# A fixed low-pass gate and four implicit convolution layers: 3x3 convolutions on sixteen 32x32 tiles in place of four 128x32 tiles

## The reference

```
Kj = K[j] - mean of each 3x3 kernel;  Lj likewise
z = conv3x3(x, Kj);  z = relu(batchnorm(z))       # "conv1"
x = x + 0.1 * conv3x3T(z, Kj)                     # "conv2"
x = batchnorm(x)
x = ifft2(fft2(x) / (0.1 * |fft2(Lj)|^2 + 1))     # "Fourier"
```

## Time and profile before

| what | us |
|---|---|
| median of 3 runs (lowest, highest) | 797.01 (794.98, 799.77) |
| the profiled execution, its own time | 796.84 |
| its span, first to last instruction | 795.0 |
| PE busy | 748.3, 94% of the span |
| DVE, ACT, POOL busy | 497.3, 449.3, 95.5 |
| share of the chain that ended last, on PE | 84% |
| of it line 873, the convolutions | 40% |

### The profile page before, as it was taken

The page is one execution under the profiler, slowest core; times in us unless marked ns, Lnnn a source line. Parts: engine busy times, 40 slices in busy tenths (PEclk is TensorE's granted clock), DMA queues, the critical chain, the costliest instruction groups (busy, mean ns, idle before and its releaser), DMA issues.

```text
span 795.0 us, 14900 instructions
## 1 busy us (share of the span) xinstructions
PE 748.3 (94%) x6016; PEld 375.6 (47%) x6016; DVE 497.3 (63%) x911; ACT 449.3 (57%) x703; POOL 95.5 (12%) x92
## 2 busy tenths in 40 slices
PE   4788999999999999999999999999999999999993
PEld 1222333222455875324558752345587632455782
DVE  2568787765957853449578534496686333966761
ACT  0456666636745765267357652683576625826773
POOL 0357766830000000000000000000000000000000
PEclk9789999999999999989999999899999998999997
DMA  9991111248000132830000328400004273000045
GB/s 184 189 153 28 28 29 28 55 91 187 2 1 1 33 77 68 193 98 2 1 1 18 93 57 191 112 1 1 2 7 103 55 183 88 1 1 2 1 100 113
DMA packets 60133, 51.16 MB, mean 64 GB/s; under 512 B 53153, under 2 KB 53282, under 8 KB 58018
## 3 DMA queue, kind: packets, MB, share of 16 engines
q1 hardware_dynamic: 54690, 48.92, 28.7%
q10 hardware_dynamic: 5376, 1.30, 1.1%
HBM read 11.92 MB, written 4.19 MB: 20 GB/s over the span
## 4 chain that ended last, share of the span: by engine, by line
PE 84%; DVE 8%; ACT 2%; issue 2%; DMA 1%; SPq 1%; POOL 0%; DVEq 0%; ACTq 0%; POOLq 0%
PE psum L873 40%; PE psum L1054 7%; PE psum L1025 7%; PE psum L947 6%; PE psum L1043 6%; PE psum L1009 5%; PE psum L896 3%; PE psum L998 3%; DVE spare L810 2%; PE psum L973 2%; PE psum L935 2%; DVE work L810 2%; PE psum L912 1%; DVE tabT L794 1%; PE psum L1018 1%
## 5 line engine op out<-in xcount | busy, mean ns | idle before, releaser
L873 PE MATMUL psum<-Z,wts 128*32 128x512 f32 x1536 | 176.7, 613 | 1.9 <-DVE Z L787 1.9
L873 PE MATMUL psum<-X,wts 128*32 128x512 f32 x1536 | 170.1, 593 | 0.2 <-DMA X<-X 0.2
L810 DVE COPY work<-psum 64x256 f32<-64x256 f32 x224 | 100.3, 448 | 22.8 <-PE psum L1009 15.9
L720 DVE BATCH_NORM_STATS2 stats<-Z 128x6 f32<-128x512 f32 x60 | 41.6, 693 | 102.2 <-ACT Z L470 101.8
L873 PEld LDWEIGHTS psum<-Z,wts 128*32 128x32 f32 x1536 | 48.9, 112 | 116.4 <-issue 107.8
L470 ACT ACTIVATE Z<-psum 128x512 f32<-128x512 f32 x64 | 38.2, 598 | 113.2 <-PE psum L873 102.1
L873 PEld LDWEIGHTS psum<-X,wts 128*32 128x32 f32 x1536 | 47.5, 109 | 105.4 <-issue 103.0
L555 ACT ACTIVATE work<-psum 64x256 f32<-64x256 f32 x160 | 83.1, 519 | 22.4 <-PE psum L1043 15.4
L530 ACT ACTIVATE Z<-Z,small 64x128 f32<-64x128 f32 (+3 forms) x92 | 84.8, 972 | 5.2 <-DVE small L778 4.7
L801 DVE SCALAR_TENSOR_TENSOR X<-psum,X 128x512 f32<-128x512 f32 x64 | 43.8, 684 | 46.6 <-PE psum L873 46.2
L542 ACT ACTIVATE work<-psum 128x512 f32<-128x512 f32 x64 | 61.1, 1108 | 8.9 <-PE psum L998 8.8
(11 more groups left out here) (104 smaller groups left out, 897.0 us busy)
## 6 DMA issues: line engine op xcount, KB each, us to landing
X<-X SPq DMA_DIRECT2D x64, 260.0 KB, 3.8
Z<-Z SPq DMA_DIRECT2D x32, 520.0 KB, 7.1
Z<-x SPq DMA_DIRECT2D x36, 128.0 KB, 4.8
out<-Z SPq DMA_DIRECT2D x60, 64.0 KB, 1.9
parS<-par SPq DMA_DIRECT2D x4, 673.0 KB, 8.2
Z<-x SPq DMA_DIRECT2D x12, 120.0 KB, 4.9
Z<-x ACTq DMA_DIRECT2D x14, 64.0 KB, 4.3
Z<-x SPq DMA_DIRECT2D x14, 64.0 KB, 4.6
```

The lines of the kernel that those rows point to most:

```text
L810: last = nc.vector.tensor_copy(dst, src)
L873: last = nc.tensor.matmul(out_b[C * r:C * r + C, :], weights[:, o:o + C], rows(src, reg, bp, g, CH, dj - 1), start=(dj == 0), stop=(dj == ...
```

## The change

**Tiles.** A convolution is done in 32x32 tiles, sixteen at a time: row quadrant q of the input times column quadrant r of the output, one tap per matmul. A block is four pieces of w groups each (w = 4, 2 or 1, so 512, 256 or 128 columns), in four banks. Its nine taps are nine passes; in each pass the four pieces (k) use different row quadrants, so that no two row tiles write the same bank and quadrant. The passes come in three phases of three column shifts. `PHASES` names for each phase and piece the copy (0 plain, 1 shifted by one row) and the row tap. Between phases PE waits for its own last matmul (the semaphore `through`), except that the one piece that stays on its tiles (`stays`) has its first pass ahead of the wait. A block is 144 matmuls, each again two pairs of instructions. Its four banks are claimed together and filled together.

**Copies and weights.** X2 and Z2 become X1 and Z1, shifted by one row: one DMA of 96 partitions and one of 32. The weights are plain taps, made by two DVE operations in place of four; the masks and windows go from the constants and from par.

**Blocks.** Conv1 of layer 0 has ten blocks: eight of w = 1 at prologue chunks 5 to 12 and two of w = 4 behind the prologue. Later conv1: w = 4, 4, 4, 2, 2. Conv2: w = 2, 2, 4, 4, 4. DVE's and ACT's work follows the pieces, so there are four copies or adds per block, of 128, 256 or 512 columns, and the last four conv1 pieces have their statistics taken from PSUM.

**Order.** The list of the layer's steps is new, and now also holds DVE's and ACT's own steps (`stats`, `relu`, `squares`, `table_sum`, `invert`, `scales`, `prepare`, `taps`). The reciprocal is cut in two of 512 columns. DVE moves eight of sixteen fwdW and eight of sixteen invH chunks (before: twelve and six). The ReLU of pair 0 is cut at group 9 instead of 4, that of the other pairs is one piece. In the last layer invH of pair 3 stands between invW of pairs 2 and 3. The prologue's own steps are as before.

```diff
--- before.py
+++ after.py
...
-BEHIND = 5
+CONV1_FIRST = [(bp, g, 1) for bp in range(2) for g in range(0, G, 4)] + [(2, 0, 4), (3, 0, 4)]
+CONV1 = [(0, 0, 4), (1, 0, 4), (2, 0, 4), (3, 0, 2), (3, 8, 2)]
+CONV2 = [(0, 0, 2), (0, 8, 2), (1, 0, 4), (2, 0, 4), (3, 0, 4)]
+AMONG = {i + 5: [i] for i in range(8)}
+LATE = [i for i in range(len(CONV1_FIRST)) if all(i not in some for some in AMONG.values())]
...
+def pieces_of(stage, j, some=None):
+    blocks = plan(stage, j) if some is None else [plan(stage, j)[i] for i in some]
+    return [(bp, g + n * k, n) for bp, g, n in blocks for k in range(4)]
...
+PHASES = (((0, 0), (0, 1), (1, 0), (1, -1)), ((0, 1), (1, -1), (0, -1), (1, 1)), ((1, -1), (1, 0), (0, 1), (0, 0)))
+def quadrants(phase, k):
+    shifted, di = PHASES[phase][k]
+    return (di - shifted) % R
+def stays(phase, k):
+    return phase > 0 and quadrants(phase, k) == quadrants(phase - 1, k)
...
+FWDW_DVE = [(bp, q) for bp in range(BP) for q in range(0, Q, 2)]
+INVH_DVE = [(bp, q) for bp in range(BP) for q in range(1, Q, 2)]
 def layer_steps(j):
-    first, second = range(0, 2), range(2, 4)
-    steps = [("table", j, 0), ("table", j, 1), ("norm", j, 1), ("table", j, 2), ("table", j, 3)]
-    after = {
-        5: fourier(j, 0, "turn"),
-        7: fourier(j, 0, "fwdW"),
-        9: fourier(j, 0, "fwdH") + fourier(j, 1, "turn"),
-        11: fourier(j, 0, "invH") + fourier(j, 1, "fwdW"),
-        13: fourier(j, 1, "fwdH") + fourier(j, 2, "turn"),
-        15: fourier(j, 1, "invH") + fourier(j, 2, "fwdW"),
-    }
-    for c in range(NCH):
-        steps += [("conv2", j, c)] + after.get(c, [])
-    steps += fourier(j, 3, "turn") + [("norm", j, 2)] + fourier(j, 2, "fwdH")
-    steps += fourier(j, 0, "invW") + fourier(j, 3, "fwdW") + fourier(j, 2, "invH") + fourier(j, 1, "invW")
-    steps += fourier(j, 3, "fwdH")
-    rest = {1: fourier(j, 3, "invH"), 3: fourier(j, 2, "invW"), 5: fourier(j, 3, "invW")}
-    for c in range(NCH):
-        if j + 1 < DEPTH:
-            steps.append(("conv1", j + 1, c))
-        steps += rest.get(c, [])
+    f = lambda what, bp: fourier(j, bp, what)
+    conv2 = lambda i: conv_steps("conv2", j, [i])
+    stats = lambda i: [("stats", j, i)]
+    conv1 = lambda i: conv_steps("conv1", j + 1, [i]) if j + 1 < DEPTH else []
+    prepare, taps = ([("prepare", j + 1)], [("taps", j + 1)]) if j + 1 < DEPTH else ([], [])
+    steps = [("table", j, 0), ("table", j, 1), ("squares", j, 0), ("norm", j, 1), ("table", j, 2), ("table", j, 3)]
+    steps += [("relu", j, 0, 0), ("squares", j, 1), ("relu", j, 0, 1), ("table_sum", j), ("relu", j, 1, 0)]
+    steps += conv2(0) + stats(0) + conv2(1) + stats(1) + [("relu", j, 2, 0), ("invert", j, 0)] + conv2(2) + stats(2)
+    steps += f("turn", 0) + [("invert", j, 1), ("relu", j, 3, 0)] + conv2(3) + f("fwdW", 0) + stats(3) + f("turn", 1)
+    steps += conv2(4) + f("fwdH", 0) + f("fwdW", 1) + stats(4) + f("turn", 2)
+    steps += f("invH", 0) + [("norm", j, 2)] + f("fwdH", 1) + [("scales", j)] + f("fwdW", 2) + prepare + f("turn", 3)
+    steps += f("invW", 0) + f("invH", 1) + f("fwdH", 2) + f("fwdW", 3) + f("invW", 1) + f("invH", 2) + f("fwdH", 3)
+    steps += conv1(0) + f("invW", 2) + f("invH", 3) + conv1(1) + taps + f("invW", 3)
+    for i in range(2, len(CONV1)):
+        steps += conv1(i)
     return steps
...
+RELU_CUTS = {0: [0, 9, G]}
+FIRST_SLOTS = (0, 1)
...
-        def shift_two(eng, dst, src, bp, done, h=None):
-            s, d, n = bp * REG, bp * REG2, G * GROUP
+        def shift_one(eng, dst, src, bp, done, h=None):
+            s, d, n = bp * REG, bp * REG1, G * GROUP
             if h is not None:
                 n //= 2
                 s, d = s + n * h, d + n * h
-            eng.dma_start(dst[0:2 * C, d + GROUP:d + GROUP + n], src[2 * C:128, s:s + n]).then_inc(done, 16)
-            eng.dma_start(dst[2 * C:128, d:d + n], src[0:2 * C, s:s + n]).then_inc(done, 16)
+            eng.dma_start(dst[0:3 * C, d + GROUP:d + GROUP + n], src[C:128, s:s + n]).then_inc(done, 16)
+            eng.dma_start(dst[3 * C:128, d:d + n], src[0:C, s:s + n]).then_inc(done, 16)
...
-                if c == NCH - 1:
-                    act.wait_ge(last_stats, j + 1)
-                nc.scalar.activation(rows(Z0, REG, c // Q, CH * (c % Q), CH), by_row(bank(n)),
+            def keep_conv1(j, bp, g, w):
+                n = NUMBER["conv1", j, bp, g, w]
+                bk.full(n)
+                if (bp, g, w) in pieces_of("conv1", j)[-4:]:
+                    act.wait_ge(last_stats, 4 * j + 1 + pieces_of("conv1", j)[-4:].index((bp, g, w)))
+                nc.scalar.activation(rows(Z0, REG, bp, g, w), by_row(bank(n)[:, 0:ROW * w]),
...
-                    for form in range(2):
-                        o = (2 * k + form) * 3 * C
-                        w = wts[:, o:o + 3 * C].rearrange("p (d o) -> p d o", o=C)
-                        m = ksum[:, C * k:C * k + C].unsqueeze(1).broadcast_to([128, 3, C])
-                        f = parS[:, P_F + o:P_F + o + 3 * C].rearrange("p (d o) -> p d o", o=C)
-                        last = nc.vector.scalar_tensor_tensor(w, in0=m, scalar=cstS[:, C_MASK + form:C_MASK + form + 1],
-                                                              in1=f, op0=ALU.mult, op1=ALU.add)
+                    o = k * TAPS * C
+                    w, f = (t[:, o:o + TAPS * C].rearrange("p (t o) -> p t o", o=C) for t in (wts, parS[:, P_K:P_GB]))
+                    m = ksum[:, C * k:C * k + C].unsqueeze(1).broadcast_to([128, TAPS, C])
+                    last = nc.vector.scalar_tensor_tensor(w, in0=m, scalar=-1.0 / TAPS, in1=f, op0=ALU.mult, op1=ALU.add)
...
+                late = i - len(pieces_of("conv1", j)) + 4
+                if late >= 0:
                     bk.full(n)
-                    nc.vector.bn_stats(stats[:, 6 * c:6 * c + 6], bank(n)).then_inc(last_stats, 1)
-                    dve.wait_ge(last_stats, j + 1)
+                    nc.vector.bn_stats(stats[:, 6 * i:6 * i + 6], bank(n)[:, 0:ROW * w]).then_inc(last_stats, 1)
+                    if late == 3:
+                        dve.wait_ge(last_stats, 4 * j + 4)
...
+                z = rows(Z1, REG1, 0, FIRST_SLOTS[1], RELU_CUTS[0][1] - FIRST_SLOTS[1])
...
+            def invert(j, i):
+                dve.wait_ge(table_summed, j + 1)
+                t = tabT[:, N * i:N * i + N]
+                nc.vector.reciprocal(t, t).then_inc(table_done, 1)
...
+            def conv2_stats(j, i):
+                for k, (bp, g, w) in enumerate(pieces_of("conv2", j, [i])):
+                    bk.result(NUMBER["conv2", j, bp, g, w])
+                    o = 6 * (4 * i + k)
+                    last = nc.vector.bn_stats(stats[:, o:o + 6], rows(X0, REG, bp, g, w))
+                if i == len(CONV2) - 1:
+                    link(last)
+                    aggregate("conv2", j)
...
-            def conv(n, c, X, X2_, weights):
-                bp, q = divmod(c, Q)
-                bk.claim(n)
-                out_b = bank(n)
-                for dj in range(3):
-                    for r in range(R):
-                        form, src, g = ((1, X2_, CH * q), (0, X, CH * q), (1, X, CH * q), (0, X2_, CH * q + 1))[r]
-                        reg = REG2 if r in (0, 3) else REG
-                        o = form * 3 * C + dj * C
-                        last = nc.tensor.matmul(out_b[C * r:C * r + C, :], weights[:, o:o + C],
-                                                rows(src, reg, bp, g, CH, dj - 1), start=(dj == 0), stop=(dj == 2),
-                                                tile_position=(0, C * r))
-                last.then_inc(filled[n % BANKS], 1)
-            def conv1(j, c):
-                if c == 0:
+            passed = []
+            def conv(step, X, XS, weights):
+                stage, j, bp, g0, w = step
+                ns = [NUMBER[stage, j, bp, g0 + w * k, w] for k in range(4)]
+                for n in ns:
+                    bk.claim(n)
+                for phase in range(3):
+                    order = sorted(range(4), key=lambda k: not stays(phase, k))
+                    for dj in range(3):
+                        for k in order:
+                            if phase and dj == 0 and k == [k for k in order if not stays(phase, k)][0]:
+                                pe.wait_ge(through, len(passed))
+                            shifted, di = PHASES[phase][k]
+                            for r in range(R):
+                                q = (r + quadrants(phase, k)) % R
+                                src, reg = (XS, REG1) if shifted else (X, REG)
+                                g = g0 + w * k + shifted + (r + di - shifted) // R
+                                tap = C * (3 * (di + 1) + dj)
+                                last = nc.tensor.matmul(bank(ns[k])[C * r:C * r + C, 0:ROW * w], weights[C * q:C * q + C, tap:tap + C],
+                                                        rows(src, reg, bp, g, w, dj - 1, C * q, C * q + C),
```

(75 more changed lines are left out.)

179 lines of the change are left out of this document (89 added, 90 removed).

## The result

The changed kernel takes 915.4 us (median of 4 runs, 909.27 to 917.19) against 796.0 us (median of 4, 792.29 to 799.77): ratio 1.149, 95% interval 1.141 to 1.156. It is slower by 119 us; the prediction was 757.0 us (729 to 787).

A forecast was written before the change was run, and what follows sets the result against it. The prediction took PE to be the bound, busy 748.3 of 795.0 us. Layers 0 to 2 (-32.7), layer 3 and the end (-10.5) and the prologue (+4.3) summed to -38.9 us from 796.84: 757 us, range 729 to 787.

The forecast's parts named there:

- rival (a): Convolution passes: a floor that width doesn't lower, from instruction starts or weight loading; +112, 869 us; chance 0.10.
- A pass of 512 columns stays 0.863 us: Convolution blocks: with sixteen tiles a pass keeps its time, so w = 4 streams for 9 x 0.863 = 7.77 us.
- the term of 8.47: Convolutions: time in us of one w = 4 block, nine passes of 0.863 plus hand-overs of 0.35.
- Blocks of w = 2 cost 4.58 us, of w = 1 2.64: Convolutions: narrow blocks stream for 3.88 and 1.94 us, plus hand-overs between phases.
- Blocks of w = 1 cost nothing: Prologue: such a block costs 2.64 us where a chunk costs 2.59; extra copies and statistics are covered.
- The shift DMAs move the same bytes and are early: Shifted copies in the layers: DMAs are early by a whole convolution; no cost counted.
- Hand-over 0.35 us: Between a block's phases: PE's wait for itself, 0.35 us each, bounds 0.10 and 0.60, 90 hand-overs.
- Norm 1 +1.45: Between conv1 and conv2, layers 1 to 3: statistics in four pieces and a longer first ReLU, +1.45 us each.
- New waits, +1.4 a layer: Layers: PE waits of 1.2, 1.0 and 0.8 us, less the present 1.6; net +1.4, bounds 0 and 6.
- Rival (b): Layers: DVE and ACT return four banks too late, three more waits of 1.75 us each; +20, 777 us; chance 0.20.
- Store tail -5.0: End of last layer: pair 2's stores run under invH of pair 3; 6.8 us fewer of stores, less 1.8.
- The rule of 25 ns per start: Matmul starts, from the Trainium skill: never closer than about 25 ns, so a pass takes at least 0.80 us; total 845.

The follow-up runs named there:

- split8_small_dma: Kernel before the change, each convolution matmul cut into eight of 64 columns, shift DMAs from layer 1 on moving one group of rows: 1095.3 us.
- w4_all: Changed kernel with blocks of w = 4 only, four per convolution, in the prologue too: 860.2 us, ratio to before 1.080.
- split4: Kernel before the change, each convolution matmul of 512 columns cut into four of 128: 842.8 us, ratio 1.059.
- narrow_old_form: Changed kernel with its blocks of w = 1 and 2 computed as 12 matmuls of 128x32 per piece: 816.0 us, ratio 1.023.

## Why the prediction was wrong

**The likeliest case fell to rival (a)**, which had 0.10: a pass has a floor that its width doesn't lower. Its break-even was F = 0.55 us per pass and its price 869 us. Measured, a pass took 1.10 us on average for w = 2 and 0.80 for w = 1 (a block's time over nine). The prediction named the start of instructions as a cause and gave it too little, since four matmuls of the earlier trace rows start 7 ns apart. Over a longer burst they don't: in split8_small_dma 128 matmuls take 2.0 us, 16 ns each, and the middle passes of w = 1 that nothing breaks take 0.43 to 0.53 us, 13 to 17 ns for each of 32 matmuls, where the change needed 6.7. Then the fetch ends the burst. Four or eight starts said nothing of the long run, and the prediction had even multiplied out the fetches (2.1 MB in place of 0.80) without dividing them by the time they had. Loading of weights, the other cause it named, was not tried by itself. Its own signs of being wrong both came: blocks of w = 2 over 6 us, a layer over 156.

**"A pass of 512 columns stays 0.863 us".** It holds for twelve tiles; with sixteen it is 1.04. Then there is the end of a block, which the prediction put at nothing: nine passes are 7.77 us, but the block of eight tiles lasts 8.61, and its last pass, one of sixteen tiles, ends 1.66 us after its start. So the term of 8.47 is 10.19 by three corrections: +0.84 for the end, +1.13 for the step from eight to sixteen tiles (8.61 to 9.74), which the look-ahead explains, -0.25 for hand-overs (0.45 for two in place of 0.70). On 23 blocks that is 40 us, the whole gain forecast. A block of w = 4 is worth 0.17 us against four chunks, not 1.9.

**"Blocks of w = 2 cost 4.58 us, of w = 1 2.64".** This is the step that failed most: w = 2 took 7.6 to 9.9 us, three times 13 to 17, and w = 1 took 5.8 to 9.0. Over the 14 and 8 blocks that is 75 and 36 us more than forecast, of the 158 by which the total missed. Each has 576 instructions on PE, which at 70 to 73 per us need 8 us however narrow they are, less what is in stock and more where the shifts run. Against the old form of the same blocks they cost 99 us.

**"Blocks of w = 1 cost nothing" in the prologue, +4.3 us.** Measured +63. The old form of the narrow blocks gives back 52 of it; in the 11.7 that it leaves, 8.6 are the two blocks behind (forecast 3.7) and 2.8 the norm (forecast 2.6; in the changed kernel itself 2.0). The -2 for chunks 13 to 15 did not come.

**"The shift DMAs move the same bytes and are early".** They are early enough for the data, but PE's fetches come late while they run. In w4_all that is 2.9 us at one pair of blocks and up to 7 us in a layer, in split4 8 to 12 us in a layer.

**Hand-over 0.35 us (bounds 0.10 to 0.60).** 0.24 us over a pass that doesn't wait: inside the bounds.

**Norm 1 +1.45.** From the last conv1 matmul to conv2 it is 6.9 us in layer 1, 6.3 in layer 2 and 6.8 in layer 3, in place of 5.6 to 5.9: +0.6 to +1.1.

**New waits, +1.4 a layer.** The sum of the layer outside the convolutions did not grow: the ten blocks of layer 1's stretch take 101.3 us in place of 82.9 for 32 chunks, 18.4 more, and the layer is 17.7 longer. Rival (b), banks, had 0.20 and three waits of 1.75 us more in each layer. The waits for DVE in front of blocks come to 2.2 us there, 1.0 of it in the norm, and narrow_old_form, whose blocks of w = 4 still claim four banks at once, has layers of 162 to 164. So banks were not the loss.

**Store tail -5.0.** Alone it is -1.4 to -2.6, with the whole new order -3.5. The forecast allowed 1.8 us until pair 3 is moved; PE waits 3.2. Its 6.8 us fewer of stores also doesn't follow from what it says: 16 stores of 0.54 us are 8.7.

**The rule of 25 ns per start** (the Trainium skill, *TensorE: Matmul & The Clock Gate*, "Wait - 56ns, not 53.3ns?") pointed the right way with the wrong number. It gave 845 us, but starts on different tiles come 16 ns apart over 128 matmuls here, so the floor of 25 ns doesn't hold across tiles. The Trainium skill's *Runtime: NRT & Kernel Launch*, section "Instruction fetch mechanics", was not drawn on; it says that the sequencer fetches blocks of 16 KiB (256 instructions) and that this is mostly hidden. The first half agrees with the 257 above. The second does not hold here: fetches come 3.3 to 4.1 us apart at best, and they were hidden only where PE used a block more slowly than that.

## What to carry to other kernels

Before cutting a matmul into more tiles or narrower columns, divide the instructions of the busiest stretch by its time. Here PE got no more than 70 to 73 per us over ten chunks even with idle DMA engines, and less while large copies ran; blocks of 59 per us ran unbroken without copies beside them. In float32 every matmul is four instructions, so sixteen tiles with 512 columns ask for 64 per 0.863 us, 74 per us: had the look-ahead not held them back, supply would have. And judge a rate from the longest run in the trace, not from its closest starts; idle time put down to "issue" in the middle of a run of matmuls is the sign, above all every 128 matmuls.

## What was not expected of the hardware

- Instructions of PE arrive 256 at a time. With DMA engines at 10 GB/s such a lot came every 3.5 to 4.1 us. In split4, with 216 and 224 GB/s of copies beside it (171.5 to 180.5 and 505.1 to 513.7 us), PE stood for 5.1 to 5.5 us after a lot that it had used in 3.7: about 9 us for each.
- Sixteen tiles run at once, but at 64 instructions a pass the next pass doesn't start in time: 1.04 us in place of 0.86. Twelve tiles (48 instructions) have no such loss, and twelve tiles are what 128x32 matmuls already fill of the array with useful work. So the fourth row quadrant gained nearly nothing here: 10.19 us in place of 10.36.
- The effect is largest in the prologue: a chunk with a block of w = 1 has over 600 instructions on PE, and the chunks, 8.7 to 9.1 us apart in before, came 12 to 20 us apart.
